# Cross-attention pipeline: scaled scores and running maximum taken one step later in VectorE's queue

## The reference, cut to what matters

```python
xn = layernorm(ctx, ln_x_g, ln_x_b)            # 8 x 1601 x 192
ln = layernorm(layernorm(x), ln_l_g, ln_l_b)   # 8 x 64 x 256
q  = ln @ Wq.T
kv = concatenate([xn @ Wkv.T, ln @ Wlkv.T], axis=1)
qn = rmsnorm(q, qn_g) * 64 ** -0.5
kn = rmsnorm(k, kn_g)                          # per head, needs the sum of squares of each key
attn = softmax(where(mask, qn @ kn.T, -big))   # over 1601 + 64 keys
out  = (attn @ v) @ Wo.T + bo
```

## Time and profile before

| | us |
|---|---|
| median of 3 runs | 519.65 (518.51 to 521.28) |
| profiled execution, its own time | 514.96 |
| its span in the trace | 513.2 |
| busy in the span: PE / DVE | 427.2 (83%) / 402.1 (78%) |
| busy in the span: ACT / POOL | 239.1 (47%) / 244.7 (48%) |
| chain that ended last: DVE / PE / POOL | 42% / 29% / 15% of the span |
| steps of the cross-attention loop | from about 47 to 340 us of the span |

### The profile page before, as it was taken

The page is one execution under the profiler, slowest core; times in us unless marked ns, Lnnn a source line. Parts: engine busy times, 40 slices in busy tenths (PEclk is TensorE's granted clock), DMA queues, the critical chain, the costliest instruction groups (busy, mean ns, idle before and its releaser), DMA issues.

```text
span 513.2 us, 6607 instructions
## 1 busy us (share of the span) xinstructions
PE 427.2 (83%) x2042; PEld 332.5 (65%) x2042; DVE 402.1 (78%) x969; ACT 239.1 (47%) x547; POOL 244.7 (48%) x248
## 2 busy tenths in 40 slices
PE   3786758788889878978989969887997789789996
PEld 0363535567767766867767758764374667568885
DVE  5846789999999999999988896425569556887776
ACT  0237744556575656755556535321242115335551
POOL 6351866658458465584575542001521331445550
PEclk9998978989999999999999999899999986999999
DMA  8604932040141131403100002910000000000001
GB/s 247 186 1 138 251 129 66 2 142 2 52 142 52 26 119 52 140 4 121 29 3 1 2 0 79 406 40 0 0 2 0 1 0 0 1 1 1 0 2 42
DMA packets 23975, 31.80 MB, mean 62 GB/s; under 512 B 2954, under 2 KB 19652, under 8 KB 23940
## 3 DMA queue, kind: packets, MB, share of 16 engines
q1 hardware_dynamic: 23940, 31.38, 19.8%
HBM read 30.69 MB, written 0.52 MB: 61 GB/s over the span
## 4 chain that ended last, share of the span: by engine, by line
DVE 42%; PE 29%; POOL 15%; issue 10%; ACT 2%; DMA 1%; SPq 1%; DVEq 0%; POOLq 0%; ACTq 0%
PE bank L571 27%; POOL kr L481 10%; DVE kss L1406 6%; DVE arena L1418 5%; DVE arena L1454 5%; DVE split_b L1397 5%; DVE cst L1343 3%; DVE arena L1613 2%; POOL crs L447 2%; DVE arena L1627 1%; DVE kguard L1409 1%; DVE big L1328 1%; DVE cmv L1347 1%; DMA mask_in<-in_p_mask 1%; DVE split_b L1687 1%
## 5 line engine op out<-in xcount | busy, mean ns | idle before, releaser
L571 PE MATMUL bank<-keyq,split_b 128*128 128x512 f32 (+2 forms) x724 | 168.4, 380 | 21.4 <-DVE split_b L1687 7.5
L571 PEld LDWEIGHTS bank<-keyq,split_b 128*128 128x128 f32 (+1 forms) x724 | 123.0, 192 | 52.3 <-issue 19.0
L481 POOL TENSOR_TENSOR kr<-kguard,neg_half 128x8 f32<-128x8 f32 (+1 forms) x56 | 93.3, 1666 | 104.6 <-DVE kguard L1409 104.4
L571 PE MATMUL bank<-arena 128*128 128x193 f32 (+4 forms) x528 | 100.0, 332 | 8.4 <-DVE arena L1613 4.4
L571 PEld LDWEIGHTS bank<-arena 128*128 128x128 f32 (+2 forms) x528 | 85.6, 192 | 18.2 <-issue 13.0
L1130 ACT ACTIVATE arena<-bank 128x512 f32<-128x512 f32 (+1 forms) x56 | 31.6, 563 | 73.4 <-PE bank L571 72.8
L571 PE MATMUL bank<-split_b,keyq 128*128 128x512 f32 x204 | 51.8, 405 | 0.0
L1397 DVE TENSOR_TENSOR split_b<-arena,split_b 32x256 fp32r<-32x256 f32 (+1 forms) x112 | 47.5, 424 | 2.5
L1418 DVE TENSOR_TENSOR arena<-bank,kr 128x512 f32<-128x512 f32 (+1 forms) x56 | 36.0, 643 | 15.3 <-POOL kr L481 15.1
L571 PEld LDWEIGHTS bank<-split_b,keyq 128*128 128x128 f32 x204 | 39.1, 197 | 7.7
L470 POOL TENSOR_TENSOR split_b<-arena,split_b 128x256 fp32r<-128x256 f32 (+1 forms) x56 | 38.4, 685 | 8.9 <-ACT split_b L1105 8.8
(11 more groups left out here) (221 smaller groups left out, 613.5 us busy)
## 6 DMA issues: line engine op xcount, KB each, us to landing
arena<-in_ctx SPq DMA_DIRECT2D x16, 576.0 KB, 4.2
arena<-in_p_ctxT SPq DMA_DIRECT2D x8, 800.5 KB, 6.4
arena<-in_p_ctxT SPq DMA_DIRECT2D x8, 400.2 KB, 7.1
arena<-in_p_experts SPq DMA_DIRECT2D x1, 2688.0 KB, 18.4
arena<-in_p_experts SPq DMA_DIRECT2D x1, 2304.0 KB, 12.1
arena<-in_p_experts SPq DMA_DIRECT2D x1, 1536.0 KB, 6.5
X<-in_x SPq DMA_DIRECT2D x1, 512.0 KB, 3.7
arena<-in_t_Wlkv SPq DMA_DIRECT2D x1, 512.0 KB, 6.9
```

What stands on the lines that cost most here:

```text
L481: pool.tensor_tensor(kr[0:r, n % 2, 0:k], kg_[0:r, n % 2, 0:k], neg_half[0:r, 0:4 * k].rearrange("p (t h) -> p t h", h=H), ALU.pow).then_i ...
L571: return nc.tensor.matmul(out_, l, r, start=start, stop=stop, skip_group_check=shared)
```

## The change

Four orders are changed; no arithmetic on the data is.

- DVE: `norm_scores` and `running_max` of group `u - 1`, not `u`, are done in step `u`, right behind `split_side(u + 2)` and ahead of `group_stats`.
- DVE: `refold_low_part` moves from the end of its step (g 0) to right behind `key_sums`; `evac_latent_out` (g 4) moves from behind `key_sums` to ahead of it.
- ACT: the twin of a refolded high part moves from g 0 to g 1.
- POOL: `context_scales` of a batch item becomes one pass over 13 columns at g 2, in place of two over 7 (g 2) and 6 (g 0).

```diff
-            def context_scales(b, part):
+            def context_scales(b):
-                pool.wait_ge(caggr, 2 * b + part + 1)
+                pool.wait_ge(caggr, 2 * b + 2)
                 k = b % 2
-                of = slice(0, 6) if part == 0 else slice(6, FULL + 1)
-                n = of.stop - of.start
-                then(pool.tensor_scalar(cve[:, k, of], cmv[:, k, of, 1], LN_EPS, None, ALU.add))
-                then(pool.tensor_tensor(crs[:, k, of], cve[:, k, of], neg_half[:, 0:n], ALU.pow))
-                if b and part == 0:
+                then(pool.tensor_scalar(cve[:, k], cmv[:, k, :, 1], LN_EPS, None, ALU.add))
+                then(pool.tensor_tensor(crs[:, k], cve[:, k], neg_half[:, 0:FULL + 1], ALU.pow))
+                if b:
                     pool.wait_ge(sdT_mm, b)
-                pool.tensor_tensor(csd[:, of], cve[:, k, of], crs[:, k, of], ALU.mult).then_inc(ctx_ready, 1)
+                pool.tensor_tensor(csd[:], cve[:, k], crs[:, k], ALU.mult).then_inc(ctx_ready, 2)
...
                 if g == 2 and b + 1 < B:
-                    context_scales(b + 1, 1)
+                    context_scales(b + 1)
                 if g == 4 and b + 1 < B:
                     sd_low(b + 1)
                 key_scales(u)
-                if g == 0 and b + 1 < B:
-                    context_scales(b + 1, 0)
...
                 last.then_inc(refold_high, 1)
-                act.wait_ge(refold_high, b - 3)
-                twin(b % 4 + 1, b % 4 + 2)
...
                 if u == 1:
                     twin(2, 5)
+                if g == 1 and 2 <= b <= 5:
+                    act.wait_ge(refold_high, b - 1)
+                    twin((b + 2) % 4 + 1, (b + 2) % 4 + 2)
...
+                if g == 4 and 2 <= b <= B + 1:
+                    evac_latent_out(b - 2)
                 if u < groups:
                     key_sums(u)
+                if g == 0 and 2 <= b <= 5:
+                    refold_low_part(b + 2)
                 if g == 3 and 2 <= b <= B + 1:
                     evac_sum(b - 2)
-                if g == 4 and 2 <= b <= B + 1:
-                    evac_latent_out(b - 2)
                 if g == 1 and 1 <= b <= B:
                     max_diagonal(b - 1)
                 if g in (2, 3) and 0 <= u - SHIFT < groups:
                     shift_scores(u - SHIFT)
                 if u + 2 < groups:
                     split_side(u + 2)
+                if 0 <= u - 1 < groups:
+                    norm_scores(u - 1)
+                    running_max(u - 1)
                 if u + LEAD < groups:
                     group_stats(u + LEAD)
-                if u < groups:
-                    norm_scores(u)
-                    running_max(u)
-                if g == 0 and 2 <= b <= 5:
-                    refold_low_part(b + 2)
```

More of the change, by code:

```diff
@@ L486, in _ @@
             then(pool.memset(wx2a[:], 0.0))
-            context_scales(0, 0)
-            context_scales(0, 1)
+            context_scales(0)
             latent_rms(0)
```

## The result

| | before | after |
|---|---|---|
| median, us | 519.37 (518.51 to 521.28, 4 runs) | 506.25 (503.30 to 509.00, 4 runs) |
| ratio | | 0.9747, 95% interval 0.9714 to 0.9779 |
| profiled execution, its own time | 514.96 | 505.19 |
| its span | 513.2 | 503.4 |
| second half's residual sum (DVE, the last of the attention) starts at | 345.98 | 336.49 |

The change is faster: by 13.1 us in the medians, by 9.8 us between the profiled executions.

A forecast was written before the change was run, and what follows sets the result against it. DVE was taken to set the pace to 254 us, PE to be fuller afterwards and in the drain. Gains of 3.9 + 0.5 + 5.3 = 9.7 us took the median from 519.65 to 510.0, range 504 to 518.

The forecast's parts named there:

- 44 to 120 us, forecast 3.9: Early loop: waits of 3.2 + 1.5 us for POOL's power vanish, less 0.8 for squares; gain 3.9 us.
- The new wait for the squares: 44 to 120 us: DVE, now ahead, meets ACT's late squares of groups 2 and 4; 0.8 us taken off.
- 120 to 254 us, forecast 0.5: Middle of the loop, DVE sets the pace: at most 1.1 us, less 0.15 a batch item; gain 0.5 us.
- at most 1.1: 120 to 254 us: ceiling of the gain, DVE's 1.1 us of waiting for POOL's power.
- the collisions: At g 0 POOL's low part meets the tail's maximum on DVE; 0.15 us lost a batch item, between nothing and 0.40.
- Nothing else of its time goes: DVE issues the same instructions, so beyond the 15.1 us wait for POOL's power none of its time disappears.
- a sign of something unseen: Middle batch items stay near 34 us apart; a fall of more than 0.5 us would mean an unseen gain.
- 254 us to the drain, forecast 5.3: After the context statistics: PE's 8.2 us of idle time closes except a 2.9 us wait; gain 5.3, bounds 2 and 8.
- below 4: Sign: PE's idle time from the first statistics-free step to the turn of the last maximum is below 4 us.
- The first rival: POOL's low part delays DVE's maximum by 0.40 us in some 40 steps: 16 us, time 526; chance 0.12.
- The second rival: PE becomes the bound, DVE waits for squares 0.2 us in each of 45 steps: 9 us, time 519; chance 0.13.
- the same difference to the median: The profiled execution before stood 4.7 us below the median; the same difference was applied to the changed kernel, giving 510.0.

The follow-up runs named there:

- the reduction: Changed kernel plus an unneeded 0.55 us DVE reduction per step: steps 14 to 41 measured 526.15 us; in another kernel, steps 43 to 55, 509.89 us.
- the deferral alone: Kernel before with only the score scaling and running maximum moved a step later on DVE: 508.48 us, ratio 0.9793.
- The cheap power: Kernel before with POOL's power of the key scales replaced by a multiplication, scores not normalised: 513.66 us, ratio 0.9891.

## Why the prediction was right

*What bounds the kernel.* Right. Where the reduction was added in the middle nearly all of it came out (14.0 of 14.9 us), in the last stretch 3.1 of 7.2; and the deferral alone gives most of the gain.

*44 to 120 us, forecast 3.9.* At item 1's maximum, at 118 us, 3.7 are gained. The new wait for the squares that was priced at 0.8 is there:

```profile
DVE kss L1402 <- ACT arena L1123: 0.8, 1, 0.8
```

*120 to 254 us, forecast 0.5.* From item 1 to item 5 the gain grows from 3.7 to 5.6, by 1.9 us; an item takes 34.0 instead of 34.5 over these four. What was wrong is "at most 1.1": it counted the wait for the power alone. Between those two maxima DVE's idle time fell from 6.95 to 5.62 us, by 1.3, which is that wait (1.3 in this stretch). Its busy time fell too, from 131.09 to 130.55, with the same 344 instructions, and although the collisions grew. The durations of the single instructions add up to more than before, 143.5 us against 143.1 (counts times means of all groups in the two stretches), while the busy time, in which overlaps count once, is less: they overlap by 1.0 us more. "Nothing else of its time goes" was wrong by that. It is spread thin, and no experiment took it apart. With 33.8 instead of 34.2 us from item to item (2 to 4) it stays just under the 0.5 us that was named as a sign of something unseen. The collisions, priced at 0.15 a batch item, were on the tail's maximum as foreseen, and dearer. The changed kernel from 117.7 to 253.8 us:

```profile
L1427 DVE TENSOR_TENSOR arena<-arena 128x512 f32<-128x512 f32 x4 | 3.0, 740 | 0.1
L1431 DVE TENSOR_TENSOR arena<-arena 65x256 f32<-65x256 f32 x4 | 2.4, 597 | 0.1
...
L1437 DVE TENSOR_TENSOR side<-arena 128x256 f32<-128x256 f32 x4 | 2.1, 530 | 0.1
```

Before, these took 692, 423 and 426 ns: 4 x (0.05 + 0.17 + 0.10) = 1.3 us, 0.3 an item.

*254 us to the drain, forecast 5.3.* From item 5's maximum on the gain grows by 3.9. The mechanism, DVE's waits closing until PE has no idle time, was right; the size of what PE keeps was not. It was put at one wait of 2.9 us for the deviations. That wait is 1.90. The 13 columns did cost what was estimated:

```profile
L445 POOL TENSOR_TENSOR crs<-cve,neg_half 128x13 f32<-128x13 f32 x7 | 17.5, 2506 | 0.6
```

But the turn of the tokens, called gone, still waits 1.80 us, since `evac_latent_out` on DVE comes as late against PE as PE has become early; and the keys behind the deviations took 3.85 us instead of 2.55, 1.3 us that no term held. From 254 to 311 us, where the last maximum is turned, PE was busy 52.93 us, so 4.1 idle: at the edge of the "below 4" that was asked for.

*The first rival,* POOL's low part on each maximum. L1429 keeps 693 ns, so it didn't happen. The cheap power shows that the mechanism is real and near: from item 1 on it cost more than the missing wait gave. That a power that ends early sets it off was read rightly.

*The second rival,* PE as the bound: 1.6 us of waits for squares, not 8. In the late steps it is half true, since only 3.1 of 7.2 us of added work came out.

*The other moves.* The merged pass was called free. From item 1 on it costs 0.6 and 1.1 us against two passes; ahead of item 1 it isn't behind, so the balance is open. Its price as foreseen was PE's later turn, inside the 5.3, and its other turns, inside PE's idle time (4.3 us in four of them, where 1.3 each had been foreseen). The latents' part ahead was counted as taking away a wait of 3.06 us; it gives 2.7 to 3.2 us from item 5's maximum to the marker. The refolded low part and the twin were not tried by themselves.

*From the sum to the median.* Span 503.4 against the 503.5 forecast, profiled execution 505.19 against 505.3: the sum was right to 0.1 us, but that is luck: two errors of 1.4 us, the middle priced too low and the end too high, cancelled. The median was forecast at 510.0 and is 506.25. What failed is the same difference to the median on both sides: of the kernel before, the profiled execution stood 4.7 us below, of the changed one 1.1. The executions of before have granted clocks from 0.944 to 0.970, and only those at 0.967 and above took under 516 us (514.96, 515.49, 515.78 in three jobs); of the changed kernel, those at 0.963 and above took 503.30 to 505.56. The means of these three and three are 515.4 and 504.7, a gain of 10.7 us; at clocks of 0.950 to 0.957 the means of eight and five executions are 518.5 and 507.3, a gain of 11.2. So at like clocks it is about 11 us, and the rest of the 13.1 goes with the draw of the executions. That the kernel before gets the higher clock more seldom, 3 times of 15 against 3 of 8, isn't shown by so few.

## What to carry to other kernels

A wait for a slow helper engine goes when its result is used one step later, if the step has room for the operands and nobody behind needs the deferred result sooner; price it by stretch, since where the other engine is nearly as full only its idle time can be had. Look next at what the deferral makes free (without it the merged pass stood in front of the power and DVE waited 19.6 us), and undo each companion of a change by itself: one was worth some 3 us in the last stretch, for another no gain was shown. Before a difference of 2 us is read from two traces, see that they begin alike. Making the helper's operation faster is not the same as hiding it: the work behind it starts earlier and may land on operations of another engine that it slows, here by 0.40 to 0.53 us each.

## What the runs showed of the hardware

POOL's power at 128 partitions took 0.71 us for 2 columns, 1.76 for 8 and 2.51 for 13; a product of 8 columns took 0.20. DVE's pair of side splits beside POOL's power took its usual 0.85 us; beside the power of the tail 1.28, beside POOL's low part 1.30, and there the shift took 1.22 instead of 0.69. Ten key matmuls took 2.5 us or 3.85 to 4.15: the slow ones came behind waits of PE of 0.89 to 2.88 us, but other waits of 1.80, 2.88 and 3.06 us were followed by fast ones.
